# Two waits of GpSimd between the gathers of a group in the attention pass, one in the tensor pass

## The reference

```
summand = _tensor_product(x[i], edge_attr, [w0, w1, w2, w3, w4])
out = jax.ops.segment_sum(summand, j, num_segments=x.shape[0])
```

```
m = jnp.maximum(jax.ops.segment_max(att, tgt, num_segments=num_nodes), 0.0)
ex = jnp.exp(att - m[tgt])
h_prime = jax.ops.segment_sum(w[:, :, None] * h_src, tgt, num_segments=num_nodes)
```

## Time and profile before

| | us |
|---|---|
| median of 3 runs | 7077.33 |
| lowest, highest | 7072.11, 7092.28 |
| the profiled execution | 7111.25 |
| its span, first to last instruction | 7109.5 |
| TensorE matmul busy | 4408.2 |
| VectorE busy | 2824.2 |
| ScalarE busy | 2273.2 |
| GpSimd busy | 3801.2 |

### The profile page before, as it was taken

The page is one execution under the profiler, slowest core; times in us unless marked ns, Lnnn a source line. Parts: engine busy times, 40 slices in busy tenths (PEclk is TensorE's granted clock), DMA queues, the critical chain, the costliest instruction groups (busy, mean ns, idle before and its releaser), DMA issues. The chain is left out here.

```text
span 7109.5 us, 95059 instructions
## 1 busy us (share of the span) xinstructions
PE 4408.2 (62%) x26265; PEld 3527.4 (50%) x26265; DVE 2824.2 (40%) x8881; ACT 2273.2 (32%) x5530; POOL 3801.2 (53%) x3904
## 2 busy tenths in 40 slices
PE   3488883566676666664555555555555555548876
PEld 2265552455565555554454444445444544435555
DVE  7875444233333333324333333333333333441114
ACT  3344442111111112123444444444444444320003
POOL 0466644666665666563555555555555545446654
PEclk6699995788788888777556555555565555669888
DMA  1233332211111112112222222222222222144442
GB/s 46 74 126 135 136 122 67 49 47 47 47 48 46 47 47 48 46 46 49 56 55 57 54 57 55 57 58 57 56 56 55 59 54 57 43 128 141 144 133 84
DMA packets 357095, 495.29 MB, mean 70 GB/s; under 512 B 198005, under 2 KB 256838, under 8 KB 345798
## 3 DMA queue, kind: packets, MB, share of 16 engines
q0 software_dynamic: 122368, 254.08, 14.3%
q1 hardware_dynamic: 232046, 237.13, 10.9%
q10 hardware_dynamic: 2400, 0.57, 0.0%
HBM read 400.97 MB, written 90.25 MB: 69 GB/s over the span
## 5 line engine op out<-in xcount | busy, mean ns | idle before, releaser
L3513 POOL DMA_INDIRECT rows_l<-table,idx_l x1568 | 1480.9, 944 | 1402.2 <-issue 1040.0
L3023 POOL DMA_INDIRECT rows_l<-table,idx_l x1344 | 1270.4, 945 | 845.3 <-issue 667.5
L1654 POOL DMA_INDIRECT rows_l<-table,row_idx x896 | 932.4, 1041 | 527.0 <-issue 249.8
L3790 PE MATMUL banks_l<-wrow_l,hot_l 128*128 128x136 f32 x3136 | 774.7, 423 | 223.0 <-ACT hot_l L3874 165.3
L3790 PEld LDWEIGHTS banks_l<-wrow_l,hot_l 128*128 128x128 f32 x3136 | 704.9, 319 | 313.8 <-issue 177.8
L3243 PEld LDWEIGHTS ps_l<-hoty_l,rows_l 128*128 128x128 f32 x2688 | 425.3, 203 | 369.4 <-issue 360.4
L3749 PE MATMUL bank_s_l<-w_edge,eT_l 128*128 128x8 f32 x1568 | 323.2, 335 | 453.5 <-issue 241.0
L3243 PE MATMUL ps_l<-hoty_l,rows_l 128*128 128x144 f32 x2688 | 471.8, 303 | 201.4 <-issue 190.0
L3749 PEld LDWEIGHTS bank_s_l<-w_edge,eT_l 128*128 128x128 f32 x1568 | 309.1, 293 | 466.4 <-issue 396.0
L3913 ACT COPY sums_l<-banks_l 128x136 f32<-128x136 f32 x196 | 53.3, 272 | 1420.2 <-DMA rows_l<-table,idx_l 791.4
L3854 ACT ACTIVATE apart_l<-iota,rel_s_l 128x128 bf16<-128x128 f32 x1568 | 497.3, 387 | 11.6 <-remote 1.6
(11 more groups left out here) (604 smaller groups left out, 7748.5 us busy)
## 6 DMA issues: line engine op xcount, KB each, us to landing
eT_l<-in_edges_laid SPq DMA_DIRECT2D x196, 256.0 KB
rows_l<-table,idx_l POOLq DMA_INDIRECT x2912
counts_table<-x_nodes SPq DMA_DIRECT2D x22, 1568.0 KB
x_nodes<-counts_table SPq DMA_DIRECT2D x22, 1568.0 KB
counts_table<-h_nodes SPq DMA_DIRECT2D x21, 1568.0 KB
h_nodes<-counts_table SPq DMA_DIRECT2D x21, 1568.0 KB
rows_l<-table,row_idx POOLq DMA_INDIRECT x896
table<-h_nodes SPq DMA_DIRECT2D x21, 448.0 KB
```

The lines of the kernel that those rows point to most:

```text
L1654: pool.indirect_dma_start(out=rows[:, slot, j, :], out_offset=None, in_=table, in_offset=bass.IndirectOffsetOnAxis(ap=what[:, j:j + 1], ax ...
L3023: pool.indirect_dma_start(out=rows[:, u, j, :], out_offset=None, in_=table, in_offset=bass.IndirectOffsetOnAxis(ap=idx[:, u, j:j + 1], axi ...
L3513: pool.indirect_dma_start(out=rows[:, u, j, :], out_offset=None, in_=table, in_offset=bass.IndirectOffsetOnAxis(ap=idx[:, u, j:j + 1], axi ...
L3790: last = nc.tensor.matmul(p_sum[:, 0:WROW], hot[:, s, j, :], wrow[:, s, j, :], start=(j == 0), stop=(j == J - 1))
```

## The change

In the tensor pass GpSimd waits between gathers 3 and 4 of a group until TensorE has summed the preceding group. In the attention pass it waits between gathers 3 and 4 until the ends of the preceding group are turned, and between gathers 5 and 6 until its carries are turned. After each wait it raises a new semaphore, `paced`, that nobody waits for. All else stays.

```diff
@@ tensor_pass @@
+        paced = sem("paced")
...
                         pool.wait_ge(summed[u], START + t)
                         pool.sem_inc(group_begun, 1)
                         for j in range(J):
+                            if j == J // 2:
+                                pool.wait_ge(summed[(u - 1) % U], START + t + (1 if u else 0))
+                                pool.sem_inc(paced, 1)
                             pool.indirect_dma_start(
@@ attention_pass @@
+        paced = sem("paced")
...
                         pool.wait_ge(weighed[u], START + t)
                         pool.sem_inc(group_begun, 1)
                         for j in range(J):
+                            if j == J // 2:
+                                pool.wait_ge(ends_turned, START + t * U + u)
+                                pool.sem_inc(paced, 1)
+                            if j == 3 * J // 4:
+                                pool.wait_ge(carries_turned, START + t * U + u)
+                                pool.sem_inc(paced, 1)
                             pool.indirect_dma_start(
```

## The result

| | before | after |
|---|---|---|
| median of 4 runs each, us | 7084.81 (7072.11 to 7103.16) | 6751.69 (6723.75 to 6763.44) |
| ratio | | 0.9512, interval 0.948 to 0.9544 |
| profiled execution: time, span | 7111.25, 7109.5 | 6749.85, 6748.0 |

A forecast was written before the change was run, and what follows sets the result against it. TensorE's results, held back by the kernel's own gathers, were taken to bound both passes. Attention -63 and tensor pass -55 sum to -118 us: 6993 from the profiled 7111.25, about 6960 by the runs' median; range 6560 to 7190.

The forecast's parts named there:

- What bounds the kernel: Both passes: TensorE's results, held back by the kernel's own gathers, released about 2.8 us after a string's last gather.
- Carries no longer late, the scan and the lifts free: Attention: carries come early in a string, so the lifts' 5.0 us delay goes; L3658 hardly waits, L3621 under 100 us.
- GpSimd pauses at both places: Attention: GpSimd pauses at both added waits, so the added semaphore increments were taken to cost nothing.
- What is late next is the scores: Attention: scores end 5.2 us into the string, are released at 9.25; period 14.2 against 14.52 us, saving 63 us.
- The beginning of the rule: Both passes: TensorE's signals are on time in the first 4.5 us or so of an unbroken string of gathers.
- The bound of 12.0 us: Attention: if the scores escape, the sums' turn is still held to 9.25 us; period 12.0 us, -494 us.
- Rival A: Gathers in short strings hold nothing back: -494 us in attention, -55 in the tensor pass, 6528 us; chance 0.20.
- the forecast's own sign: Attention: if L3551, VectorE's wait for the scores, waits less than 3 us a group, the short-strings rival holds.
- Tensor pass, -55: Tensor pass: 12.47 us a group falls to 11.9, -96 us, against 41 us of waits for landings; net -55 us.
- Rival B, the lost lead: Both passes become one chain of gather, landing, TensorE, signal: attention +163, tensor pass +138, 7378 us; chance 0.22.
- A release at 3.95 us: Both passes: held signals come 3.95 us after the last gather instead of 2.8, costing each group 1.15 us more.
- Issue early, wait late: Skill's rule on DMAs, against the change: 2.0 us exposed in every group would be 728 us more; not followed.

The follow-up runs named there:

- e13: The kernel before with only gathers 0 to 3 of each attention group from the second round on, no wait added: 6182.90 us, 0.8697 of the kernel before.
- e6: The change, its attention waits being for increments by TensorE's instruction queue and for group k-2, not k-1: 7087.24 us, 0.9983 of the kernel before.
- e9: The change with its own lead, its attention waits being for increments by TensorE's instruction queue, not completions: 7042.70 us, 0.9913 of the kernel before.
- e12: The change without the attention wait for the ends, on the third chip: 7064.77 us, 0.9942 of the kernel before.
- e14: The change without SyncE's loads of edges, tables and gates in attention from the second round on: 6642.91 us, 0.9354 of the kernel before.
- e2: The change with the tensor pass's wait alone, on the first chip: 5520.54 us, 1.0002 of the kernel before.
- e11: The change with its two attention waits alone, on the third chip: 6851.66 us, 0.9632 of the kernel before.
- e8: The change with one attention wait, for the ends, ahead of gather 0 in place of its two: 7064.80 us, 0.9941 of the kernel before.
- e10: The change waiting in attention for the same completions, but of group k-2 in place of k-1: 6907.70 us, 0.9730 of the kernel before.
- e1: The change with its two attention waits alone, on the first chip: 5535.50 us, 1.0029 of the kernel before.
- e3: The change without the attention wait for the carries, on the first chip: 5535.02 us, 1.0030 of the kernel before.
- e4: The change without the attention wait for the ends, on the first chip: 5538.54 us, 1.0035 of the kernel before.

## Why the prediction was right and wrong

- **What bounds the kernel.** Right: TensorE's completions are held back by strings of gathers (e13), and are released 2.6 to 2.8 us after the last one. That the named releaser, a landing, is not the cause holds after as well: L3613 waits for no rows.
- **Carries no longer late, the scan and the lifts free.** Right: the lifts wait for nothing, the scan for 6 us.
- **GpSimd pauses at both places.** Wrong: it pauses ahead of gather 4 alone. That strings of sixteen are gone is not the gain either: e6, e9 and e12 have nearly all strings of eight too, at 0.9983, 0.9913 and 0.9942.
- **What is late next is the scores, held to 9.25 us, in nearly every group, over 1000 us; period 14.2.** This is the step that failed. They are held to the string's end in the fourth group alone (9.65 us after the carries, 15.0 us a group). In the other three they are taken at 3 to 7 us, and all the waits for them are 341.0 + 227.3 + 38.8 = 607 us. The beginning of the rule, on time in the first 4.5 us and then not until the end, was read from few rows, and both halves of it are false: scores done inside the first 4.5 us are late, and a late signal can come through in the midst. SyncE's loads are one thing that keeps it from doing so (e14). The place of the scores was off as well: 5.2 us into the string was forecast, 3.7 to 4.5 was measured (medians of the four groups of a round), since gather 4 goes only 1.7 to 2.1 us ahead of the turned carries, not 2.6. Put there, the scores would have been on time by the forecast's own rule.
- **The bound of 12.0 us.** It describes the three quick groups: the sums' turn held, VectorE's steps on them at 9.6 to 9.9 us after the carries, the next carries at 12.0 to 12.4. (12.0 + 12.4 + 12.4 + 15.0) / 4 = 12.95, the measured 12.91. So 313 us in place of 63. The forecast had this chain and put the scores ahead of it. Rival A gave this bound, but its reason, that short strings hold nothing back, is false: L3613's 475 us are held signals. By the forecast's own sign (under 3 us a group at L3551) it didn't hold either: 607 / 196 is 3.1.
- **Tensor pass, -55.** Right in sign, about half the size: 26 us. The 12.47 us a group from which it started was misread, since its row ended two groups early: it is (3257.1 - 1154.3) / 167 = 12.59, and 12.44 after. The 18 us that e2 and e11 were expected to show rest on the same row. Forecast was 11.9 and 41 us for landings; TensorE's sums after wait 502.9 us in 342 waits that the trace puts down to landings, 8.9 us before. Which part of the difference is theirs no run separates.
- **Rival B, the lost lead.** A release at 3.95 us didn't appear in the strings of at most eight that were read. In e8, with the lead gone altogether, landings are waited for, beside scores that are held.
- **Issue early, wait late** (the Trainium skill, DMA: Bandwidth & Descriptors, section Rules for kernel authors). With one group more lead e10 has 0.973, where e11, with less than the change, has 0.9632 on the same chip; where no signal is held back the short lead costs 0.3% (e1, e3, e4). The rule holds on the first chip and not on the others.

## What to carry to other kernels

Where an engine is late although its producer's work was done, look at what a third engine was issuing between the two times, not at the releaser that the table names. A pause in a string of transfers can be worth more than the lead it costs, if it lies between a held result and its user, and if what ends it is a signal of the kind that is held back. Count the pauses in the trace, too: of two waits that were added here, one made them all. And time such a change on more than one chip: here its sign hangs on that.

## What was not expected of the hardware

One program took 5518 us on one chip and 7081 to 7115 us on three others. In attention a group of the kernel with the tensor wait alone takes 9.95 us on the first, and the kernel before took 14.52 in the profile of this case. The tensor pass is shorter there too, 1680.5 us from first sum to last in e2 against 2076.8 after. On the others the times of SyncE's own instructions spread as well (6 to 1374 ns against 29 always), which suggests, and doesn't show, that the hold is not TensorE's alone. The granted clock differs, 0.64 in e1's attention pass and 0.56 in that of after, but e13 reached 9.78 us a group at 0.61 on a chip of the other kind. What in the chips makes the difference was not found.
